# A two-layer AdaLN kernel: projection jobs of the attention stage behind its weightings, and token maxima spread by way of DRAM

## The chip, the cores and the metric

The kernel runs on one core of one Trainium2 chip. The metric is the device time of one execution in microseconds (us), a median over several runs. TensorE (PE) does the matrix products and the transposes, VectorE (DVE) and ScalarE (ACT) the elementwise work and the reductions, GpSimd (POOL) a few elementwise operations and the gathers. SyncE (SP) issues most of the transfers.

## The reference, cut to what matters

Two batches of 2048 tokens with 256 features go through two layers. The change lies in the two parts of the first layer.

```
# layer 0, attention: position i sees the positions j >= i - 16
h   = layernorm(x) * (1 + ca) + sa
q, k, v = h @ Wq.T + bq, h @ Wk.T + bk, h @ Wv.T + bv
att = softmax(where(j >= i - 16, q @ k.T / sqrt(256), -1e30))
x   = x + ga * ((att @ v) @ Wo.T + bo)

# layer 0, soft mixture: 8 experts of 128 slots
xn, se   = rms_norm(layernorm(x) * (1 + cb) + sb), rms_norm(slot_embeds)
logits   = xn @ se.T                       # per batch [2048 tokens, 1024 slots]
dispatch = softmax(logits, over the tokens)
combine  = softmax(logits, over the slots)
slots    = dispatch.T @ xn
y        = gelu(slots @ w1) @ w2
x        = x + gb * (combine @ y)
```

Behind it comes the second layer: a state-space block with a scan, then a mixture with a choice of tokens by each expert. The change leaves both alone.

## The kernel before, in words

The instructions of each engine are written out by hand, one program for each engine, and semaphores tie them together. An engine works through its own program in order. The program is cut into stages; the attention takes about the first 370 us of the span, the soft mixture the next 510 us.

**Attention (`attention`).** The rows of queries are cut into 32 tiles of 128, 16 for each batch, and taken from the last to the first, one in each step n from 0 to 31. Because a query sees all later keys, tile n of a batch sees 2 key tiles at first and 16 in the end. The kernel keeps scores in blocks of 512 keys, so a step has 1 to 4 blocks. In step n, PE does this, in order: the projection jobs of the step (`jobs_of(n)`), the transposes of the first three blocks of probabilities of row n (L469), the scores of row n + 1 (`scores`, into b_pS), and then the weightings of row n, one for each block (`weighted`, into b_pO), with the transpose of a fourth block behind the first of them. fp32 products are made of three products of high and low parts (`exact_matmul`, L61 to L63).

A job is something that PE puts into one of three slots of the PSUM tile b_pT and that is then taken out in two parts: ACT copies the high part (`high`), and DVE subtracts it from the same slot and keeps the low part (`low`). The kinds are "m" (modulation vectors, L369 and L371), "k" (a group of four tiles of h turned over, L408, low part on L661), "q" (low part on L663), "v" (low part on L668), "e" (slot embeddings turned over, L416, low part on L673) and "t" (a block of probabilities, high part on L544, low part on L676). Slots are used in turn: a job waits until the low part of the job three places earlier is out. A group's k jobs stand in step user - 3 and its q and v jobs in step user - 2, where user is the first step that reads the group. That gives these projection jobs: steps 0 to 3 have modulation jobs; steps 0, 4, 8, 13, 16, 20 and 24 have two k jobs; steps 1, 5, 9, 14, 17, 21 and 25 have two q and two v jobs; steps 27 to 30 have one e job each.

ACT does in step n: `high` of the projection jobs and of the first three blocks, the exponentials of row n + 1 (L553, which wait for DVE's maximum b_nmax), some squares, and `high` of a fourth block. DVE does in step n: `low` of the same jobs, the maxima of row n + 1 (`maxima`, L685 to L694), `low` of a fourth block, then side work that stands at fixed steps, and last `update` of row n (L700 to L707: reciprocal, row added to x, statistics), which waits for PE's last weighting. The side work is `group_scaled` (L622, steps 3, 7, 12, 15, 19, 23), `key_part` (L635 to L638, steps 2, 5, 9, 14, 17, 21, 25), `group_centred` (L614, steps 2, 6, 11, 14, 18, 22), `stats` (L715 to L725, steps 1, 4, 8, 10, 13, 16), and from step 24 `modulate` and `finish_row` of the rows of the next stage.

**Soft mixture (`soft_mixture`).** For each batch b the logits of all 8 experts are kept in SBUF (d_raw, 8 tiles of 128 slots by 2048 tokens). `tops` takes the maximum over the experts into d_top, so that what is left is a maximum over the 128 partitions for each token. For each half of 8 token tiles, PE transposes d_top into d_pT (`turn_tops`, L1811), DVE reduces it to one column for each tile (`row_tops`, L1231, into d_rmax), PE multiplies each column, spread over 128 columns, by the identity (`spread_tops`, L1818), and ACT copies the result back into d_top (L1582), where each partition now has the maxima of all tokens. DVE then subtracts d_top from the logits of each expert (`shift`, L1236), ACT takes the exponentials, and PE combines. Beside this chain PE works on the experts: `hidden` (8 tiles for experts 0 to 3, then 8 for 4 to 7) and `outputs` (one for each expert, into two halves of d_pO). `outputs` of expert et waits until DVE has taken expert et - 2 out (`processed`, L1240), and on DVE `processed(0)` stands behind `shift(0)`, `processed(1)` behind `shift(1)`, and so on. In batch 0 both `hidden` and `outputs` are products of high and low parts, in batch 1 plain fp32.

Of the kernel before, what the change touches and what calls it, by code (L numbers as in the profile page):

```python
# [4 lines left out]
F32 = mybir.dt.float32  # L5
# [7 lines left out]
P = 128  # L13
# [95 lines left out]
def attention(nc, m, w):  # L109
# [3 lines left out]
    with ExitStack() as ctx:  # L113
# [109 lines left out]

        jobs = [j for n in range(-1, NT) for j in jobs_of(n) + probs_of(n)]
        at = {j: i for i, j in enumerate(jobs)}
# [128 lines left out]
        def _(pe):  # L354
# [130 lines left out]
            for n in range(-1, NT):  # L485
                for job in jobs_of(n):
                    kinds[job[0]](job)
                    if job == ("m", 1, 0):
                        output_weights()
                probs = probs_of(n)  # L490
                for job in probs[:EARLY]:
                    transposes(job)
                if n + 1 < NT:
                    scores(n + 1)
                for i, job in enumerate(probs):
                    weighted(job)
                    if i + EARLY < len(probs):
                        transposes(probs[i + EARLY])

        @block.scalar  # L500
        def _(act):
# [70 lines left out]
            for n in range(-1, NT):  # L572
                probs = probs_of(n)
                for job in jobs_of(n) + probs[:EARLY]:
                    high(job)
                    if job == ("m", 1, 0):
                        act.wait_ge(s["fold_ps"], 1)
                        nc.scalar.copy(raw_wvo, by_two(pS[:, 0:GW])).then_inc(s["raw_done"], 1)
                        nc.scalar.copy(m.vrow[:], over(pS[:, GW:GW + C], B)).then_inc(s["raw_done"], 1)
                        nc.scalar.copy(wr[:], pS[:, GW + C:2 * GW]).then_inc(s["raw_done"], 1)  # L580
                    if job == ("k", 0, CH - 1):
                        weights_high(0)
# [4 lines left out]
                if SQUARES_AT <= n < SQUARES_AT + E:  # L587
# [4 lines left out]
                    nc.scalar.activation(junk[:], m.se[:, e], ACT.Square, accum_out=ss[:, e:e + 1]).then_inc(s["squared"], 1)  # L592
                for job in probs[EARLY:]:
                    high(job)
# [7 lines left out]
        def _(dve):  # L602
# [175 lines left out]
            for n in range(-1, NT):  # L778
                probs = probs_of(n)
                for job in jobs_of(n) + probs[:EARLY]:  # L780
                    low(job)
# [10 lines left out]
                if tiles_of_step(n - 2):  # L792
                    clamp(tiles_of_step(n - 2))
                for job in probs[EARLY:]:
                    low(job)
# [45 lines left out]
def soft_mixture(nc, m, w):  # L841

    with ExitStack() as ctx:
# [62 lines left out]
                                    for n, shape, o in (("uh", [P, 2, 2, C], 0), ("un", [P, 2, 2, C], 4 * 4 * C), ("ug", [P, 2, CH, 2 * P], 8 * 4 * C),  # L906
                                                        ("umod", [P, 3, C], 12 * 4 * C), ("ubout", [P, C], 15 * 4 * C))]
        third = placed("uh_third", [P, 2, C], area + 10 * KB)
        rows_of = lambda b, q: third[:] if b and q == PAIRS - 3 else uh_[b][:, q % 2]
# [10 lines left out]
                 "l_ready part_done max_done nmax_done exp_done raw_done top_done t_ready t_copied_a t_copied_d sl_ready rsum_done sl_scaled "  # L920
                 "h_ready h_done y_ready y_done ones_done mt_ready rmax_done mb_ready mb_done shifted p_done o_ready "
                 "crs_done x_done w_in x_out x_back st_done small_in mods_in u_bias u_chain u_pow "
# [69 lines left out]
        def _(sp):  # L992
# [11 lines left out]
            def turned_out(b, q):  # L1004
                await_copy(sp, at[b, "u", q, 0])
                cols = slice((b * NTB + 2 * q) * P, (b * NTB + 2 * q + 2) * P)
                sp.dma_start(m.uT_dram[:, :, cols], ug[b][:, q % 2]).then_inc(u_out[q % 2], 16)

            feed_forward(0)
            sp.wait_ge(s["x_out"], 16)  # L1010
            sp.wait_ge(s["y_ready"], E)
# [16 lines left out]
            for k in range(2):  # L1028
                sp.dma_start(wout[k][:], w["W_out"].rearrange("(k h p) n -> k p h n", p=P, h=2)[k]).then_inc(s["wout_in"], 16)
            for q in range(PAIRS - 3, PAIRS):  # L1030
                turned_out(0, q)
            for k in range(2):
                sp.wait_ge(u_out[k], 16 * PAIRS // 2)
# [98 lines left out]
        def _(dve):  # L1132
# [95 lines left out]
            def row_tops(b, h):  # L1228

                dve.wait_ge(s["mt_ready"], b * 2 + h + 1)  # L1230
# [175 lines left out]
            for b in range(B):  # L1406
# [45 lines left out]
                row_tops(b, 1)  # L1452
                for e in range(ES):
# [71 lines left out]
        def _(act):  # L1525
# [133 lines left out]
            for b in range(B):  # L1659
# [23 lines left out]
                for j in range(HT):  # L1683
                    gelu(b, 0, j)
                    if not b:
                        hidden_high(0, j)
                    if not b and j == 2:
                        slots_high_of(1)
                    if j == 4:
                        spread_tops(b, 0)  # L1690
                spread_tops(b, 1)
                if b:
# [35 lines left out]
        def _(pe):  # L1728
# [74 lines left out]
            def turn_tops(b, h):  # L1803
# [4 lines left out]
                else:  # L1808
                    pe.wait_ge(s["mb_done"], b * 2 + h)
                for t in range(NH):  # L1810
                    last = nc.tensor.transpose(pT[:, t // 4, t % 4 * P:(t % 4 + 1) * P], top[:, (h * NH + t) * P:(h * NH + t + 1) * P], m.ident[:])  # L1811
                last.then_inc(s["mt_ready"], 1)

            def spread_tops(b, h):
                pe.wait_ge(s["rmax_done"], b * 2 + h + 1)
                for t in range(NH):
                    col = h * NH + t
                    last = nc.tensor.matmul(pT[:, t // 4, t % 4 * P:(t % 4 + 1) * P], rmax[:, col:col + 1].to_broadcast([P, P]), m.ident[:],  # L1818
                                            start=True, stop=True)
                last.then_inc(s["mb_ready"], 1)  # L1820

# [47 lines left out]
            for b in range(B):  # L1869
# [34 lines left out]
                for j in range(HT):  # L1904
                    hidden(b, 0, j)
                    if j == 3:
                        spread_tops(b, 0)
# [4 lines left out]
                spread_tops(b, 1)  # L1912
# [1412 lines left out]
def program(nc, a, out):  # L3325
# [5 lines left out]
    m.y_dram = nc.dram_tensor("y_dram", [P, NT, C], F32).ap()  # L3331
    m.cum_dram = nc.dram_tensor("cum_dram", [NT * HEADS, P], F32).ap()
    m.bb_dram = nc.dram_tensor("bb_dram", [2, DT0], F32).ap()
    m.decayed = 2
# [114 lines left out]
```

## Time and profile before

| what | value |
|---|---|
| median of 3 runs | 1689.68 us (1688.67 to 1689.85) |
| profiled execution, its own time | 1690.98 us |
| span of the profiled execution | 1689.2 us |
| mean granted TensorE clock | 0.987 of full speed |
| PE busy | 1598.3 us, 95% |
| DVE busy | 1196.2 us, 71% |
| ACT busy | 779.8 us, 46% |

The profile is that of one execution. What it gives as busy is time in which an instruction of that engine ran; a PE instruction's end is modelled and overlaps the next one's start by up to 0.2 us, so the next start is the better mark. Times of instructions are microseconds from the start of the span, and 1.8 us of the execution's own time lie outside the span.

### The profile page before, as it was taken

What the parts mean: (1) busy time and instruction counts of PE and PEld (TensorE: products, weight loads), DVE (VectorE), ACT (ScalarE), POOL (GpSimd) and SP (SyncE); (2) the same over time, 40 slices, a digit from 0 to 9 for tenths busy, and PEclk for the clock granted to TensorE, in tenths of its full rate; (3) what the DMA queues carried; (4) which work ended last, traced back from release to release, by engine and by line L of the source; (5) the groups of instructions that cost most, each with busy time, mean ns of one, the idle gap of its engine ahead of it and who ended that gap; (6) DMA issues with size and microseconds to landing.
All of it is one profiled execution on the core that took longest, in us unless ns stands there. A gap on an engine that the chain in (4) does not pass through costs nothing. (4 is left out here: it accounts for less than half of the span.)

```text
span 1689.2 us, 25755 instructions
## 1 busy us (share of the span) xinstructions
PE 1598.3 (95%) x9282; PEld 1367.1 (81%) x9282; DVE 1196.2 (71%) x2655; ACT 779.8 (46%) x1529; POOL 582.0 (34%) x475
## 2 busy tenths in 40 slices
PE   6899989989999999999979999999889999999996
PEld 4689878888888888867867888888678778888896
DVE  6877688764567756646886898998877836666663
ACT  3333333344357134436237777778421314454542
POOL 2100020000000003322436777777400024777764
PEclk9999999999999999999988999999999999999999
DMA  7000000010010000111015222222241125565653
GB/s 230 5 1 1 1 1 1 1 51 1 1 50 4 23 13 20 66 57 69 28 59 207 73 91 78 78 79 82 69 149 51 50 65 172 136 168 144 147 119 38
DMA packets 80538, 113.14 MB, mean 67 GB/s; under 512 B 16014, under 2 KB 60186, under 8 KB 80028
## 3 DMA queue, kind: packets, MB, share of 16 engines
q1 hardware_dynamic: 66460, 93.00, 17.1%
q0 software_dynamic: 12288, 17.31, 5.7%
q8 instruction: 75, 1.23, 0.3%
q10 hardware_dynamic: 1664, 1.18, 0.2%
q14 instruction: 51, 0.42, 0.1%
HBM read 83.17 MB, written 27.68 MB: 66 GB/s over the span
## 5 line engine op out<-in xcount | busy, mean ns | idle before, releaser
L2001 POOL DMA_INDIRECT k_xe<-rows_dram,idx x64 | 82.3, 1286 | 179.0 <-DVE idx L3073 140.7
L3140 POOL DMA_INDIRECT out<-k_eo,idx x64 | 117.0, 1828 | 74.5 <-DVE k_eo L3236 57.3
L1830 PE MATMUL d_pO<-d_sp,d_raw 128*128 128x257 f32 x512 | 116.1, 384 | 1.9 <-DVE x L1248 1.7
L1830 PEld LDWEIGHTS d_pO<-d_sp,d_raw 128*128 128x128 f32 x512 | 96.8, 192 | 16.5 <-DVE x L1248 2.4
L553 ACT ACTIVATE b_p<-b_pS,b_nmax 128x384 f32<-128x384 f32 (+16 forms) x32 | 38.1, 1190 | 131.7 <-DVE b_nmax L694 131.7
L61 PE MATMUL b_pO<-b_vh,b_ph 128*128 128x256 f32 x302 | 87.8, 291 | 7.0 <-DVE b_pl L676 6.8
L62 PE MATMUL b_pO<-b_vh,b_pl 128*128 128x256 f32 x302 | 85.3, 282 | 0.0
L63 PE MATMUL b_pO<-b_vl,b_ph 128*128 128x256 f32 x302 | 85.3, 282 | 0.0
L347 POOL TENSOR_TENSOR x<-x,b_vrow 128x256 f32<-128x256 f32 x32 | 24.2, 786 | 168.8 <-DVE b_hs L622 168.7
L2217 ACT ACTIVATE g_dlm<-d_cumb,mod 128x128 f32<-128x128 f32 x256 | 78.5, 395 | 1.2 <-DMA d_cumb<-cum_dram 1.2
L3195 ACT ACTIVATE k_act_g<-k_pg 128x512 f32<-128x512 f32 x64 | 38.3, 599 | 87.3 <-PE k_pu L63 87.0
L3253 DVE TENSOR_TENSOR k_hid<-k_act_g,k_pu 128x512 f32<-128x512 f32 x64 | 44.0, 688 | 42.8 <-ACT k_act_g L3195 42.2
L1567 ACT COPY d_raw<-pL 128x512 f32<-128x512 f32 x64 | 37.3, 586 | 79.7 <-PE pL L63 79.7
L61 PE MATMUL k_po<-k_wh,k_hh 128*128 128x256 f32 x256 | 72.4, 283 | 0.6 <-issue 0.6
L63 PE MATMUL k_po<-k_wl,k_hh 128*128 128x256 f32 x256 | 72.5, 283 | 0.0
L62 PE MATMUL k_po<-k_wh,k_hl 128*128 128x256 f32 x256 | 72.4, 283 | 0.0
L2831 ACT ACTIVATE i_act_g<-i_pg 128x512 f32<-128x512 f32 x30 | 17.9, 598 | 114.2 <-PE i_pu L63 114.2
L676 DVE TENSOR_TENSOR b_pl<-b_pT,b_ph 128x512 fp32r<-128x512 f32 (+3 forms) x86 | 50.3, 618 | 24.0 <-ACT b_ph L544 24.0
L61 PE MATMUL b_pS<-b_kh,b_qh 128*128 128x512 f32 (+5 forms) x172 | 65.8, 383 | 1.4 <-DVE b_vl L668 1.4
L61 PEld LDWEIGHTS b_pO<-b_vh,b_ph 128*128 128x128 f32 x302 | 57.6, 191 | 10.5 <-DVE b_pl L676 10.2
L685 DVE TENSOR_REDUCE b_part<-b_pS 128x1 f32<-128x512 f32 (+4 forms) x86 | 49.8, 587 | 22.0 <-PE b_pS L63 21.8
L1118 POOL MEMSET d_sp<- 128x4 f32 x4 | 0.3, 105 | 181.8 <-PE pL L63 167.6
(583 smaller groups left out, 5495.5 us busy)
## 6 DMA issues: line engine op xcount, KB each, us to landing
d_cumb<-cum_dram SPq DMA_DIRECT2D x32, 512.0 KB, 4.2
k_wf<-in_WgT SPq DMA_DIRECT2D x16, 512.0 KB, 4.0
k_wf<-in_WuT SPq DMA_DIRECT2D x16, 512.0 KB, 4.9
k_wf<-in_WdT SPq DMA_DIRECT2D x16, 512.0 KB, 6.9
rows_dram<-h_hx SPq DMA_DIRECT2D x32, 136.0 KB, 3.9
x<-in_x SPq DMA_DIRECT2D x8, 512.0 KB, 10.4
d_w<-in_w SPq DMA_DIRECT2D x4, 1024.0 KB, 6.3
uT_dram<-d_ug SPq DMA_DIRECT2D x16, 256.0 KB, 2.4
```

What stands on the lines that cost most here:

```text
L61: nc.tensor.matmul(out, ah, bh, start=start, stop=False)
L62: nc.tensor.matmul(out, al, bh, start=False, stop=False)
L63: return nc.tensor.matmul(out, ah, bl, start=False, stop=stop)
L553: nc.scalar.activation(pr[:, n % 2, off:w], pS[:, bank[n] + off:bank[n] + w], ACT.Exp, bias=nmax[:, n % 2:n % 2 + 1], scale=scale, accum_o ...
L676: nc.vector.tensor_tensor(pl[:, r, 0:w], src[:, 0:w], ph[:, r, 0:w].bitcast(F32), ALU.subtract).then_inc(s["lo_done"], 1)
L685: nc.vector.reduce_max(part[:, n % 2, g:g + 1], pS[:, bank[n] + g * GW + skipped(n, g):bank[n] + g * GW + width(n, g)], axis=AX).then_inc( ...
L1830: last = nc.tensor.matmul(pO[:, t % 2, 0:PW], raw[e][:, t * P:(t + 1) * P], proc[e], start=e == 0, stop=e == E - 1)
L2001: nc.gpsimd.indirect_dma_start(out=m.xe[:, e % 2, t, :], out_offset=None, in_=m.rows, in_offset=bass.IndirectOffsetOnAxis(ap=column(m, e, ...
L2217: nc.scalar.activation(le[:, b, h, :], cumb[:, b, h, :], ACT.Relu, bias=cs[:, b, 3, h:h + 1], scale=-1.0).then_inc(s["dd_done"], 1)
L3140: nc.gpsimd.indirect_dma_start(out=out, out_offset=bass.IndirectOffsetOnAxis(ap=column(m, e, t), axis=0), in_=eo[:, e % 2, t, :], in_offse ...
L3195: nc.scalar.activation(act_g[:, f % 2], pg[:, f % 2], ACT.Gelu).then_inc(s["gelu_done"], 1)
L3253: nc.vector.tensor_tensor(hid[:, f % 2], act_g[:, f % 2], pu[:, f % 2], ALU.mult).then_inc(s["hid_done"], 1)
```

## The change

In the attention, the last projection jobs of a step move from the head of the step to behind its weightings, one behind each. The number of jobs that move is at most the number of blocks of the row. So in steps 3, 4, 8, 13, 14, 20, 24 and 27 to 30 all of them move, in steps 5 and 21 the two v jobs, in steps 9 and 25 all but the first q job, in steps 0, 1, 2, 16 and 17 only the last job. The three engines and the turn of the slots keep one common order. On ACT the moved jobs stand behind the exponentials of row n + 1, on DVE behind its maxima and ahead of the side work and the update.

In the mixture, PE's products with the identity and ACT's copies go (`spread_tops`). Both halves are now turned over and reduced early (the second behind the fourth `hidden` tile). PE turns d_rmax over with one transpose behind the seventh `hidden` tile, DVE keeps the 16 by 128 result in SBUF (`keep_tops`), and SP writes it to DRAM (8 KB) and, when that has landed, reads it back into all 128 partitions of d_top (1024 KB). `shift(0)` waits for that transfer. In batch 1 the two transfers stand on SP's queue ahead of the last turned pair (`turned_out(0, PAIRS - 1)`).

```diff
-        jobs = [j for n in range(-1, NT) for j in jobs_of(n) + probs_of(n)]
+        def ahead_of(n):
+            own, probs = jobs_of(n), probs_of(n)
+            return own[:max(len(own) - len(probs), 0)]
+
+        def between(n, i):
+            probs, later = probs_of(n), jobs_of(n)[len(ahead_of(n)):]
+            return probs[i + EARLY:i + EARLY + 1] + later[i:i + 1]
+
+        def behind(n):
+            return [j for i in range(len(probs_of(n))) for j in between(n, i)]
+
+        jobs = [j for n in range(-1, NT) for j in ahead_of(n) + probs_of(n)[:EARLY] + behind(n)]
...
@@ PE
-                for job in jobs_of(n):
+                for job in ahead_of(n):
                     kinds[job[0]](job)
...
                 for i, job in enumerate(probs):
                     weighted(job)
-                    if i + EARLY < len(probs):
-                        transposes(probs[i + EARLY])
+                    for later in between(n, i):
+                        if later[0] == "t":
+                            transposes(later)
+                        else:
+                            kinds[later[0]](later)
@@ ACT, and the same with low(job) on DVE
-                for job in jobs_of(n) + probs[:EARLY]:
+                for job in ahead_of(n) + probs[:EARLY]:
                     high(job)
...
-                for job in probs[EARLY:]:
+                for job in behind(n):
                     high(job)
@@ soft mixture, SP
+        token_tops = eT[0][0:NTB, 0:P]
+            def spread_tops(b):
+                sp.wait_ge(s["tops_kept"], b + 1)
+                sp.dma_start(m.tops_dram, token_tops).then_inc(s["tops_in"], 16)
+                sp.wait_ge(s["tops_in"], 32 * b + 16)
+                sp.dma_start(top[:], m.tops_dram.rearrange("t n -> (t n)").partition_broadcast(P)).then_inc(s["tops_in"], 16)
...
-            for q in range(PAIRS - 3, PAIRS):
+            for q in range(PAIRS - 3, PAIRS - 1):
                 turned_out(0, q)
+            spread_tops(1)
+            turned_out(0, PAIRS - 1)
@@ soft mixture, DVE
+            def keep_tops(b):
+                dve.wait_ge(s["mt_ready"], b * 3 + 3)
+                nc.vector.tensor_copy(token_tops, pT[0:NTB, 0, 0:P]).then_inc(s["tops_kept"], 1)
...
                 if e == 0:
-                    dve.wait_ge(s["mb_done"], (b + 1) * 2)
+                    dve.wait_ge(s["tops_in"], 32 * (b + 1))
@@ soft mixture, ACT
-            def spread_tops(b, h):
-                act.wait_ge(s["mb_ready"], b * 2 + h + 1)
-                nc.scalar.copy(top[:, h * HALF:(h + 1) * HALF], pT[:].rearrange("p s n -> p (s n)")).then_inc(s["mb_done"], 1)
@@ soft mixture, PE
-            def spread_tops(b, h):
-                pe.wait_ge(s["rmax_done"], b * 2 + h + 1)
-                for t in range(NH):
...
+            def turn_token_tops(b):
+                pe.wait_ge(s["rmax_done"], b * 2 + 2)
+                nc.tensor.transpose(pT[0:NTB, 0, 0:P], rmax[:], m.ident[:]).then_inc(s["mt_ready"], 1)
...
                     hidden(b, 0, j)
                     if j == 3:
-                        spread_tops(b, 0)
+                        turn_tops(b, 1)
+                    if j == 6:
+                        turn_token_tops(b)
                 if b:
                     pe.wait_ge(s["h_done"], b * SH * HT + HT)
-                turn_tops(b, 1)
-                outputs(b, 0)
-                spread_tops(b, 1)
-                for et in range(1, ES):
+                for et in range(ES):
                     outputs(b, et)
                 if b:
-                    pe.wait_ge(s["mb_done"], 2 * B)
+                    pe.wait_ge(s["tops_kept"], B)
```

## Rows read from the trace of the kernel before

**Rows 1.** The page, busy time, share of the span and instructions of each engine

```profile
PE 1598.3 (95%) x9282; PEld 1367.1 (81%) x9282; DVE 1196.2 (71%) x2655; ACT 779.8 (46%) x1529; POOL 582.0 (34%) x475
```

**Rows 2.** Busy time by stretches: start:end, length, then each engine's busy us

```profile
52.00:74.00 22.00, 18.16 (x104) 12.03 (x103) 19.63 (x63) 7.01 (x18) 4.97 (x6) 1.00 0.03 8
...
140.00:164.00 24.00, 24.00 (x173) 22.65 (x172) 15.13 (x42) 8.56 (x20) 0.00 (x0) 1.00 0.00 1
```

**Rows 3.** PE's waits from 0 to 390 us: in total, times, longest

```profile
PE b_pO L61 <- DVE b_pl L676: 6.8, 12, 1.4
PE b_pT L408 <- DVE b_hs L622: 4.8, 4, 1.4
PE b_pT L469 <- DVE o_sel L673: 4.6, 4, 1.8
PE b_pT L469 <- DVE b_kl L661: 3.8, 5, 1.3
...
PE b_pT L61 <- DVE b_kl L661: 1.7, 1, 1.7
```

**Rows 4.** Timeline of PE, steps 16 to 18: start, length, in brackets the idle before

```profile
221.22 0.39 PE L61 MATMUL b_pO<-b_vh,b_ph 128*128 128x256 f32 x1 [0.32 <-DVE b_pl L676]
...
223.21 0.63 PE L469 MATMUL b_pT<-ident,b_p 128*128 128x128 f32 x4 [0.66 <-ACT b_p L553]
...
226.15 0.39 PE L61 MATMUL b_pO<-b_vh,b_ph 128*128 128x256 f32 x1 [0.46 <-DVE b_pl L676]
```

**Rows 5.** Timeline of DVE in steps 16 and 17

```profile
213.21 0.21 DVE L694 TENSOR_SCALAR b_nmax<-b_lifted,b_along 128x1 f32<-128x1 f32 x1
213.34 1.40 DVE L715 BATCH_NORM_STATS2 st<-x 128x6 f32<-128x256 f32 x4
...
215.55 0.15 DVE L700 RECIPROCAL b_rden<-b_esum 128x1 f32<-128x1 f32 x1
...
216.87 1.40 DVE L663 SCALAR_TENSOR_TENSOR b_ql<-b_pT,qb,b_qh 128x512 fp32r<-128x512 f32 x2
```

**Rows 6.** Timeline of ACT in steps 16 and 17

```profile
210.02 1.07 ACT L523 CAST b_kh<-b_pT 128x512 fp32r<-128x512 f32 x2 [3.49 <-PE b_pT L408]
...
213.46 0.58 ACT L553 ACTIVATE b_p<-b_pS,b_nmax 128x384 f32<-128x384 f32 x1 [2.09 <-DVE b_nmax L694]
```

**Rows 7.** DVE by line, 0 to 370 us: busy us, mean ns, idle before

```profile
L704 DVE SCALAR_TENSOR_TENSOR x<-b_pO,b_rden,x 128x256 f32<-128x256 f32 x32 | 15.5, 484 | 11.4 <-PE b_pO L63 9.7 <-POOL x L347 0.8
...
L614 DVE SCALAR_TENSOR_TENSOR b_hs<-x,mean,mod 128x256 f32<-128x256 f32 x32 | 13.4, 481 | 0.2 <-DVE mod L647 0.2
...
L635 DVE SCALAR_TENSOR_TENSOR b_hw<-b_hs,wr 128x256 f32<-128x256 f32 x32 | 13.3, 471 | 0.0
```

**Rows 8.** Timeline of PE, the mixture in batch 1 and then in batch 0

```profile
741.77 1.95 PE L1818 MATMUL d_pT<-ident,d_rmax 128*128 128x128 f32 x16
...
751.27 1.09 PE L1811 MATMUL d_pT<-ident,d_top 128*128 128x128 f32 x8 [0.69 <-ACT d_work L1578]
...
761.37 7.17 PE L1795 MATMUL d_pO<-d_w,d_work 128*128 128x256 f32 x32 [0.31 <-DVE d_sp L1240]
...
515.31 0.39 PE L61 MATMUL d_pO<-d_w2h,d_hid_high 128*128 128x256 f32 x1 [0.94 <-DVE d_sp L1240]
```

**Rows 9.** Timeline of DVE, the first subtraction of each batch

```profile
512.63 2.29 DVE L1236 TENSOR_TENSOR d_raw<-d_raw,d_top 128x2048 f32<-128x2048 f32 x1 [3.19 <-ACT d_top L1582]
...
758.68 2.29 DVE L1236 TENSOR_TENSOR d_raw<-d_raw,d_top 128x2048 f32<-128x2048 f32 x1 [5.06 <-ACT d_top L1582]
```

**Rows 10.** Transfers: queue, count, KB each, median us from issue to landing

```profile
x<-x_dram SPq DMA_DIRECT2D x1, 1024.0 KB, 5.0
...
d_wide_bias<-in_b_in SPq DMA_DIRECT2D x1, 512.0 KB, 3.7
...
cum_dram<-d_cumT SPq DMA_DIRECT2D x1, 64.0 KB, 1.7
...
cum_dram<-d_cumT SPq DMA_DIRECT2D x1, 8.0 KB, 2.0
```

More of the change, by code:

```diff
@@ L779, in _ @@
                 probs = probs_of(n)
-                for job in jobs_of(n) + probs[:EARLY]:
+                for job in ahead_of(n) + probs[:EARLY]:
                     low(job)
@@ L793, in _ @@
                     clamp(tiles_of_step(n - 2))
-                for job in probs[EARLY:]:
+                for job in behind(n):
                     low(job)
@@ L920, in soft_mixture @@
                  "l_ready part_done max_done nmax_done exp_done raw_done top_done t_ready t_copied_a t_copied_d sl_ready rsum_done sl_scaled "
-                 "h_ready h_done y_ready y_done ones_done mt_ready rmax_done mb_ready mb_done shifted p_done o_ready "
+                 "h_ready h_done y_ready y_done ones_done mt_ready rmax_done tops_kept tops_in shifted p_done o_ready "
                  "crs_done x_done w_in x_out x_back st_done small_in mods_in u_bias u_chain u_pow "
@@ L1007, in turned_out @@
                 sp.dma_start(m.uT_dram[:, :, cols], ug[b][:, q % 2]).then_inc(u_out[q % 2], 16)
+            def spread_tops(b):
[3 more added lines that the diff above has]
+                sp.dma_start(top[:], m.tops_dram.rearrange("t n -> (t n)").partition_broadcast(P)).then_inc(s["tops_in"], 16)
             feed_forward(0)
+            spread_tops(0)
             sp.wait_ge(s["x_out"], 16)
@@ L1228, in row_tops @@
             def row_tops(b, h):
-                dve.wait_ge(s["mt_ready"], b * 2 + h + 1)
+                dve.wait_ge(s["mt_ready"], b * 3 + h + 1)
                 nc.vector.tensor_reduce(rmax[:, h * NH:(h + 1) * NH], pT[:].rearrange("p s (t n) -> p (s t) n", n=P), AX, ALU.max).then_inc(s["rmax_done"], 1)
+            def keep_tops(b):
+                dve.wait_ge(s["mt_ready"], b * 3 + 3)
+                nc.vector.tensor_copy(token_tops, pT[0:NTB, 0, 0:P]).then_inc(s["tops_kept"], 1)
             def shift(b, e):
                 if e == 0:
-                    dve.wait_ge(s["mb_done"], (b + 1) * 2)
+                    dve.wait_ge(s["tops_in"], 32 * (b + 1))
                 nc.vector.tensor_tensor(raw[e][:], raw[e][:], top[:], ALU.subtract).then_inc(s["shifted"], 1)
@@ L1451, in _ @@
                             slots_low(1)
-                row_tops(b, 1)
+                        if j == 3:
+                            row_tops(b, 1)
+                        if j == 5:
+                            keep_tops(b)
+                else:
+                    row_tops(b, 1)
+                    keep_tops(b)
                 for e in range(ES):
@@ L1688, in _ @@
                         slots_high_of(1)
-                    if j == 4:
-                        spread_tops(b, 0)
-                spread_tops(b, 1)
                 if b:
@@ L1808, in turn_tops @@
                 else:
-                    pe.wait_ge(s["mb_done"], b * 2 + h)
+                    pe.wait_ge(s["rmax_done"], b * 2 + h)
                 for t in range(NH):
@@ L1812, in turn_tops @@
                 last.then_inc(s["mt_ready"], 1)
-            def spread_tops(b, h):
-                pe.wait_ge(s["rmax_done"], b * 2 + h + 1)
-                for t in range(NH):
[L1817 to L1820, printed above, removed]
+            def turn_token_tops(b):
+                pe.wait_ge(s["rmax_done"], b * 2 + 2)
+                nc.tensor.transpose(pT[0:NTB, 0, 0:P], rmax[:], m.ident[:]).then_inc(s["mt_ready"], 1)
             def combine(b, t):
@@ L1906, in _ @@
                     if j == 3:
-                        spread_tops(b, 0)
+                        turn_tops(b, 1)
+                    if j == 6:
+                        turn_token_tops(b)
                 if b:
                     pe.wait_ge(s["h_done"], b * SH * HT + HT)
-                turn_tops(b, 1)
-                outputs(b, 0)
-                spread_tops(b, 1)
-                for et in range(1, ES):
+                for et in range(ES):
                     outputs(b, et)
                 if b:
-                    pe.wait_ge(s["mb_done"], 2 * B)
+                    pe.wait_ge(s["tops_kept"], B)
                     state_turn(0, PAIRS - 1)
@@ L3332, in program @@
     m.cum_dram = nc.dram_tensor("cum_dram", [NT * HEADS, P], F32).ap()
+    m.tops_dram = nc.dram_tensor("tops_dram", [NTB, P], F32).ap()
     m.bb_dram = nc.dram_tensor("bb_dram", [2, DT0], F32).ap()
```

## The prediction

> **What bounds the kernel now.** The page comes first: PE is busy for 95% of the span, DVE for 71% [rows 1], so an edit pays only where PE waits. The busy time by stretches shows two kinds of attention step: where a row has 13 or more key tiles, PE has no gap and DVE works 15.13 of 24 us; in the short rows of the start PE works 18.16 of 22 us and DVE 19.63 of 22 [rows 2]. There DVE is close to being the bound itself. The list of PE's waits names what the change aims at: 4.8 us for h scaled (L622), 4.6 for the e jobs' low parts, 3.8 for the k jobs' [rows 3], each because the transposes of a new row stand right behind projection jobs and need their slots. The biggest entry, 6.8 us for b_pl [rows 3], is PE ready to weight while DVE has not got to the low part of the probabilities. What keeps DVE from it is the DVE order: side work, update, then the low parts of the next row. For the mixture I read PE's timeline around L1818 and the first subtraction on DVE [rows 8, 9].
>
> **The attention: what is removed.** The moved work is the same work, no instruction more. What can go are the waits at projection jobs. Step 4's and 20's k jobs no longer stand ahead of DVE's scaled h, and in steps 27 to 30 the third transpose no longer waits for an e job: 4.6 us [rows 3], of which nearly all comes back, since there the e job is alone and has two or three weightings behind it.
>
> **The attention: what is added.** DVE now meets a moved job in the place of the fourth block, ahead of side work and update. In short rows that job's product runs on PE only behind the weighting, so DVE idles for it, and what stood in that gap before (side work) comes after. Who waits for it: the low parts of the next row behind the update, and behind them PE's next weighting. Three prices go into it. From the end of a job on PE to its low part out is 1.45 us: ACT 0.6 and DVE 0.7 with the handoffs (two ACT copies take 1.07 us [rows 6], two DVE low parts 1.40 [rows 5]; the one place in the trace where nothing hides it shows 1.65 [rows 3]). Side work: 2.2 for statistics (213.34 to 215.55 [rows 5]), four times 0.4 for centring, four times 0.43 for the key part (means of 481 and 471 ns that overlap the next [rows 7]). The update takes 1.05: 0.15 [rows 5], 0.48 [rows 7], and a statistics instruction, of which L715 has four in 1.40 [rows 5].
>
> Worked for steps 16 to 18. Before, DVE had b_nmax out at 213.42 and started the statistics at once [rows 5]. After, only one k job stands ahead, DVE is through with the maxima at 212.85, and PE weights from 211.75 (half a microsecond earlier) and turns the second k job over until 213.1. ACT takes the exponentials first (0.58 and 0.19 behind b_nmax [rows 6]) and a square of 0.6, so the copy runs until 214.65 and the low part is out at 215.35: DVE has stood idle for 1.85, and PE, which used to start the q jobs at 213.1, starts at 215.45. Behind it DVE needs 2.2 + 1.05 + 0.35 for statistics, update and slot scales (218.9), then four low parts of 2.55 in all: row 17's are out at 221.4, against 221.22 for the weighting before [rows 4]. The last v job now follows that weighting and ends at 224.05, and row 18 is turned over from there (223.21 before [rows 4]). In step 17 DVE idles again from 222.65 to 224.75, has v's low part at 225.4, and needs 1.75 + 1.05 + 0.4 + 0.6 for key part, update, embedding and low part: row 18 is weighted from 229.2 instead of 226.15 [rows 4]. Steps 16 to 18 lose 3.05 us.
>
> The same sum, step by step, gives for the other groups:
> - Steps 0 to 7: DVE idles 2.65, 2.1 and 1.7 us in steps 2, 3 and 4 behind m and k jobs and then has 3.35, 2.3 and 2.2 of side work; PE's q job of step 5 waits 1.9 for k's low part. Set against that are 1.05 us won by step 2 and the waits that go. Net 5.4 lost. These are the short rows where DVE had no room [rows 2].
> - Steps 8 to 10: q waits 0.7 for k, the third transpose of step 9 waits 1.6 for q's low part, which stands behind statistics and update; less 0.5 that goes. Net 1.9 lost.
> - Steps 13 to 15: four blocks a row. PE gains 3.1 us by step 15, but DVE has key part and centring (3.35) behind the last v job, so the first weighting of step 15 comes when it came before. Net 0.
> - Steps 20 to 23: the scaled-h wait goes (1.3), q waits 1.8 for k, key part and update come late, and with them maxima and exponentials of row 23. Net 2.25 lost.
> - Steps 24 to 30: 0.7 gained in step 24, used up by late DVE work in 26 (the exponentials of row 27 come 1.3 late), then 4.2 gained at the e jobs. Net 3.3 gained.
>
> Sum: 5.4 + 1.9 + 0 + 3.05 + 2.25 - 3.3 = 9.3 us slower. The bounds: if other gaps of DVE absorb half of each loss, 3; if every moved job costs PE the full 1.65 [rows 3], 13.
>
> **The mixture.** Each `spread_tops` is 16 PE instructions, 1.95 us [rows 8] with 1.8 to the next start; the ACT copy behind it, 1.0, is seen by PE only through `shift(0)`. Added are one transpose (0.15), a DVE copy of 16 by 128 (no row has it; between 0.15 for a column and 0.4 for 128x256, I take 0.25), and two transfers one behind the other. Writing 8 KB lands after 1.7 to 2.0 us, reading 1024 KB to the same layout after 5.0 [rows 10]. That the source is one row for all partitions shows no extra price: 512 KB of that kind took 3.7 [rows 10]. I take 1.8 + 5.2 with 0.2 for handoffs, 7.2; bounds 6.7 and 9. The Trainium skill (DMA: Bandwidth & Descriptors, section Anatomy of one DMA) gives an estimate of 2.0 us fixed plus bytes over 436 GB/s, 2.0 and 4.4 here; by it the sum would be 0.6 us better in each batch. Its fixed part agrees with the rows, its rate is better than the 5.0 us row.
>
> Batch 0: PE ends the fourth `hidden` tile at 498.7, turns the second half (0.95) and does three more tiles of 1.4, so it is through the seventh at 503.9. DVE keeps the maxima at 504.4, d_top is back at 511.6, against 512.63 [rows 9]. The third `outputs` product stands 2.68 behind that start (515.31 [rows 8]) and starts at 514.3. PE reached it 0.9 early before and now waits 2.7 there: the 3.5 us of products removed turn into waiting, 1.0 is gained. All that follows hangs on that product and shifts with it.
> Batch 1: the fourth tile ends at 741.77 [rows 8], the transposes take 0.95, three tiles 1.76 each; DVE has free hands, so the maxima are kept at 748.55 and d_top is back at 755.75 (758.68 [rows 9]). PE starts `outputs` without the transposes in front (751.27 [rows 8]) at 750.75, is through two at 3.45 each at 757.65, and goes on at 758.45 instead of 761.37 [rows 8]: 2.9 gained. SP is idle in both windows, and the transfer put behind waits for ACT until long after. Bounds: 0 and -1 with the slow transfers, 1.9 and 3.7 with the fast, so the mixture gives -1 to 5.6, taken as 4.0.
>
> **Sum.** 9.3 - 4.0 = 5.3 us slower than the profiled execution's 1690.98, which lies 1.3 above the median of the runs; against the median 1689.68, 1695.0.
>
> **The rivals.** A run of this kernel can tell about 0.2%, 3.4 us.
> - DVE's late side work is mostly absorbed: the losses of steps 0 to 23 halve to 6.3, less 3.3, and the mixture gives 4: 1 us faster, 1688.7. For it speaks that DVE idles 24 us in front of low parts over the stage; against it that the short rows have only 2.4 us of 22 free [rows 2]. Chance 0.22.
> - Faster: DVE finishes its side work before the low parts are needed. Then the waits for L622, L673 and L661 go (4.8 + 4.6 + 3.8 [rows 3]), k to q costs 1.5 in five steps, and the mixture gives 4: 1690 - 13.2 + 7.5 - 4 = about 1680. It decides from the point where side work, update and one low part (up to 5 us) fit into PE's transposes and scores; they take 2 to 3 us in the short rows and 6 to 7 in the long. Chance 0.15.
> - The transfers are slow, say 9 us in each batch (another read delayed on the same engines): PE waits at the third product, the mixture gives -1, the whole is 10 slower, 1700. The other transfers of this stage are over by then. Chance 0.08.
> - The forecast, 1691 to 1699: chance 0.55.
>
> **How the numbers follow.** The forecast's range comes from attention 5 to 12 and mixture 2.5 to 5. The first rival and the lower edge of the forecast lie within 0.2%: 0.22 and a seventh of 0.55, 0.30. Slower is 0.55, faster 0.15. From 1686 to 1700 leaves out the faster rival and the far end of the slow transfers.
>
> **What would show it.** In the trace after: DVE idles in front of L661, L668 and the modulation lines in steps 2 to 5, 8, 9, 16, 17, 20 and 21, and PE's waits for b_pl rise above 6.8 and those for b_kl at the first q product above 1.7, while those for b_hs and o_sel are gone. The attention ends some 9 us later, near 378. In the mixture, L1818 and L1582 are gone, PE waits about 2.7 us at the third product of batch 0 and 0.8 in batch 1, and the two transfers take about 7 us from `keep_tops`. The prediction is wrong if the stage ends no later than before, or if the read of 1024 KB takes far from 5 us.

## The result and the profile after

The changed kernel takes 1702.32 us (median of four runs, 1701.01 to 1705.55) against 1689.40 for the kernel before: ratio 1.0077, 95% interval [1.0065, 1.0089]. It is 12.9 us slower, where 5.3 were forecast, and the time lies above the forecast's 1691 to 1699. Timed once more on another chip, beside a kernel before of 1691.42, it took 1702.5 (1.0059 [1.0044, 1.0073]).

The profiled execution took 1701.01 us, its span is 1698.3, 9.1 longer than before. Read first: does the attention end later? The last update of a row on DVE (first line before, second after):

```profile
368.91 0.48 DVE L704 SCALAR_TENSOR_TENSOR x<-b_pO,b_rden,x 128x256 f32<-128x256 f32 x1 [1.44 <-PE b_pO L63]
```
```profile
381.88 0.48 DVE L720 SCALAR_TENSOR_TENSOR x<-b_pO,b_rden,x 128x256 f32<-128x256 f32 x1 [1.44 <-PE b_pO L63]
```

12.97 us later, against 9.3 forecast. So the stages behind gained 3.9, against 4.0. What PE waits for in the attention, to be held against [rows 3] (in total, times, longest):

```profile
PE b_pO L61 <- DVE b_pl L692: 14.3, 11, 3.9
PE b_pT L61 <- DVE b_kl L677: 8.6, 6, 2.1
PE b_pT L384 <- ACT b_cs L586: 7.3, 1, 7.3
PE b_pT L482 <- ACT b_p L569: 3.7, 5, 0.8
PE b_pS L61 <- DVE b_vl L684: 3.4, 4, 1.4
PE b_pT L482 <- DVE b_ql L679: 2.4, 3, 1.3
PE b_pT L482 <- DVE b_vl L684: 1.6, 3, 0.5
PE b_pT L421 <- DVE b_hs L638: 1.4, 1, 1.4
```

The waits that were to go went: b_hs from 4.8 to 1.4, o_sel from 4.6 to nothing. What came in their place is b_pl, 6.8 to 14.3, and b_kl in front of the first q product, 1.7 to 8.6. (L384 is the start of the kernel and is there before as well.) These are the waits that were forecast. But what came and what went do not add up to 13 us. The next view shows what is missing. PE's busy time in the whole stage, before and then after (start:end, length, the busy time of PE with its instructions and of the other engines, granted clock as a share of full, DMA share, GB/s):

```profile
0.00:370.10 370.10, 331.30 (x2196) 290.82 (x2196) 272.77 (x738) 133.51 (x272) 48.01 (x63) 1.00 0.09 28
```
```profile
0.00:383.10 383.10, 338.29 (x2196) 297.25 (x2196) 269.84 (x738) 131.97 (x272) 48.13 (x63) 0.97 0.08 27
```

The same 2196 instructions keep PE busy 7.0 us longer. Only 6.0 of the 13 us are idle time; the rest is slower work, and the third column from the end points to the reason: the granted clock is 0.97 instead of 1.00. Some of this lies ahead of the first moved jobs. In the first 45 us, before and after:

```profile
0.00:45.00 45.00, 29.52 (x132) 20.21 (x133) 28.05 (x81) 13.97 (x28) 12.31 (x22) 1.00 0.66 216
```
```profile
0.00:45.00 45.00, 32.57 (x133) 22.71 (x134) 27.94 (x81) 14.35 (x29) 12.29 (x22) 0.92 0.66 216
```

So 3.0 of the 7.0 us of slower work belong to the start and 3.9 to the rows behind it. Where the clock falls there is seen in PE's timeline at the two places that my sum for steps 16 to 18 was about:

```profile
211.84 0.58 PE L61 MATMUL b_pO<-b_vh,b_ph 128*128 128x256 f32 x1 [3.58 <-DVE b_pl L692]
212.22 0.42 PE L62 MATMUL b_pO<-b_vh,b_pl 128*128 128x256 f32 x1
212.44 0.42 PE L63 MATMUL b_pO<-b_vl,b_ph 128*128 128x256 f32 x1
...
214.14 0.41 PE L62 MATMUL b_pO<-b_vh,b_pl 128*128 128x256 f32 x1
214.36 0.41 PE L63 MATMUL b_pO<-b_vl,b_ph 128*128 128x256 f32 x1
...
226.05 0.47 PE L61 MATMUL b_pT<-b_kh,wqkh 128*128 128x512 f32 x1 [2.14 <-DVE b_kl L677]
```

PE stood 3.58 us for the low part of row 15, and then each product comes 0.21 us behind the one before. The twelve products of the block take 2.9 us. After the 2.14 us wait the products are slow too, from half a microsecond behind it, and the two q jobs and the v job of step 17 take 5.99 us (4.30 before). PE alone in slices of 2 us (busy time, granted clock, DMA share, GB/s):

```profile
212.00:214.00 2.00, 2.00 (x10) 0.50 0.00 0
214.00:216.00 2.00, 2.00 (x11) 0.50 0.00 0
216.00:218.00 2.00, 2.00 (x18) 0.91 0.00 0
226.00:228.00 2.00, 1.95 (x6) 0.65 0.00 0
228.00:230.00 2.00, 2.00 (x7) 0.50 0.00 0
230.00:232.00 2.00, 2.00 (x17) 0.99 0.00 0
```

0.50 is 1.2 instead of 2.4 GHz. The Trainium skill (TensorE: Matmul & The Clock Gate, Part 1) says that a gate sets PE's clock to half or full by how busy PE has been recently; these rows agree.

In the mixture, DVE's first subtraction of each batch answers to [rows 9], and the transfers to my term from [rows 10] (queue, size, us to landing; batch 0, then batch 1's read). The last two lines are PE's third product of batch 0 and of batch 1:

```profile
523.90 2.29 DVE L1266 TENSOR_TENSOR d_raw<-d_raw,d_top 128x2048 f32<-128x2048 f32 x1 [3.67 <-DMA d_top<-tops_dram]
...
767.30 3.16 DVE L1266 TENSOR_TENSOR d_raw<-d_raw,d_top 128x2048 f32<-128x2048 f32 x1 [6.04 <-DMA d_top<-tops_dram]
```
```profile
d_top<-tops_dram SPq DMA_DIRECT2D x1, 1024.0 KB, 4.9
tops_dram<-mod SPq DMA_DIRECT2D x1, 8.0 KB, 1.4
```
```profile
d_top<-tops_dram SPq DMA_DIRECT2D x1, 1024.0 KB, 4.6
```
```profile
526.58 0.39 PE L61 MATMUL d_pO<-d_w2h,d_hid_high 128*128 128x256 f32 x1 [2.71 <-DVE d_sp L1270]
...
770.85 7.17 PE L1824 MATMUL d_pO<-d_w,d_work 128*128 128x256 f32 x32 [0.32 <-DVE d_sp L1270]
```

1.4 and 4.9 us, in all 6.3 from the maxima kept (6.0 in batch 1), against 7.2 forecast. Counted from the end of the attention, the third product of batch 1 comes 3.5 us sooner (770.85 less 761.37 [rows 8], less 12.97).

### The profile page after: what moved, and what is told of

It reads as the page before. It is cut to its first block and busy times, and to the rows that moved or that the text cites. A ratio compares the mean times of both kernels' runs of the same rounds, so it can differ in the third digit from the quotient of the medians.

```text
span 1698.3 us, 25632 instructions
## 1 busy us (share of the span) xinstructions
PE 1598.1 (94%) x9220; PEld 1366.2 (80%) x9220; DVE 1192.5 (70%) x2657; ACT 775.0 (46%) x1525; POOL 577.6 (34%) x475
## 5 line engine op out<-in xcount | busy, mean ns | idle before, releaser
L61 PE MATMUL b_pO<-b_vh,b_ph 128*128 128x256 f32 x302 | 89.8, 297 | 14.4 <-DVE b_pl L692 14.3
L2632 PE MATMUL g_py<-g_wide,g_dlm 128*128 128x64 f32 x512 | 61.2, 273 | 0.8 <-POOL g_wide L2153 0.7
```

Of the source, the lines that this page charges most:

```text
L61: nc.tensor.matmul(out, ah, bh, start=start, stop=False)
L2632: last = nc.tensor.matmul(py[:, h * HD:(h + 1) * HD], mt[:, h, :], dtx[:, b, h * HD:(h + 1) * HD], start=True, stop=True)
```

## The experiments

Ratios are to the kernel before on the same chip. To compare stages I take one mark for each step, the start of the DVE instruction that adds a row to x (L704 before), and write down how much later than before it is in the profiled execution (us). The labels are those of the experiments below:

```
row updated   0     4     7    10    15    18    23    30    31   ends stage
changed     +1.2  +6.2  +7.7  +9.3 +10.8 +15.6 +17.6 +13.0 +13.0
e10 again   +3.2  +9.0 +10.5 +12.1 +13.5 +18.3 +20.4 +15.7 +15.7
e1 att.     +3.4 +11.5 +13.0 +14.6 +16.1 +20.9 +23.0 +18.3 +18.3
e8 filled   +0.3  +4.0  +5.5  +7.2  +6.6  +9.7 +11.8  +7.1  +7.1
e4 DVE      +0.1  -3.4  +0.3  +1.3  -1.6  +2.1  +2.8  -2.9  -2.9
e7 k ahead  +3.2  +5.3  +5.9  +6.8  +3.9  +3.3  +3.9  -1.1  -1.1
e5 chosen   +0.4  +1.6  +1.6  +1.6  -1.3  -1.3  -1.3  -7.2  -7.2
e3 e jobs   -0.3  -0.3  -0.3  -0.3  -0.3  -0.4  -0.4  -6.3  -6.3
e6 long     -0.3  -0.2  -0.3  -0.3  -3.1  -3.2  -3.2  -9.1  -9.1
e9 best     +0.7  -2.7  -2.7  -2.7  -5.6  -5.6  -5.6 -11.6 -11.6
```

**Each part alone** (e1, e2). The first seven hunks of the diff, and the others.

> The attention part alone, the mixture as before. The trace of the changed kernel has the attention ending 13.0 us later and the rest gaining about 4. If the two parts are independent, this kernel takes 1689.4 + 13 = 1702 to 1705 us, and with the mixture part alone the two differences add up to that of the whole change (12.9 us between the medians). Rival: the parts act on each other (a late attention changes when the mixture's loads land, or the granted clock of what follows); then this one would come out at the time of the whole change, 1702, or above 1707.

> The mixture part alone, the attention as before. By the prediction's term it gains 4.0 us: 1685.4. The traces so far show the first batch 1.7 us shorter up to the third output product, and a granted clock that falls after the wait in front of that product in the second batch. Rival: those clock losses eat the gain, and this kernel is within 1.5 us of 1689.4. A third product of batch 0 that waits 2.7 us and one of batch 1 that waits 0.3 to 0.8 would be the same in either case; what differs is the clock after them.

Measured: the attention part 1706.82 us (1.0093 [1.0078, 1.0108]), the mixture part 1687.31 (0.9983 [0.9971, 0.9995]), before 1690.39. +16.4 and -3.1 make +13.3, where the whole change gave +12.9: the parts are independent as far as these intervals can tell, which is some 3 us. The attention part lies above the 1702 to 1705 that I expected, the mixture part 1.9 us above its 1685.4. The mixture's gain is between 0.8 and 4.9 us by its interval, so its sign is confirmed, and 4.0 is not excluded. Its rival, that a lower clock eats the gain, falls: from 390 to 910 us the granted clock is 0.97 in the kernel before, in the changed kernel and in this one.

The attention part's runs spread over 6 us (1704.23 to 1710.43), and its profile, of the slowest of them, ends the stage 18.3 us late instead of 13.0. It shows one reason. Behind the same wait of 2.03 us in step 4, PE runs the same 26 instructions at full clock in the changed kernel (first line) and partly at half in this one (second):

```profile
80.00:85.00 5.00, 3.29 (x26) 1.00 0.10 28
```
```profile
84.00:89.00 5.00, 4.77 (x26) 0.66 0.11 28
```

So the same wait can cost the clock in one execution and not in another.

**Only the e jobs moved** (e3). In the changed kernel:

```
 own, probs = jobs_of(n), probs_of(n)
+if n < TURN_AT:     # 27
+    return own
 return own[:max(len(own) - len(probs), 0)]
```

> Only the e jobs of steps 27 to 30 are moved behind weightings, all other projection jobs stand ahead as before; the mixture part is in. The prediction had 4.2 us of gain at the e jobs and 4.0 in the mixture, and put all the loss into steps 0 to 26: 1681 to 1683. Rival 1: the e jobs' gain came only because rows 27 to 30 were late anyway; then 1685. Rival 2: moved jobs cost something at the e jobs as well: 1687 or more.

Measured 1681.19 (0.9945 [0.9932, 0.9957]), as expected. The stage ends 6.3 us sooner than before, 5.9 of it gained in steps 27 to 30. Where nothing late stands behind a moved job, the move pays more than the waits for o_sel had in the table (4.6).

**DVE's order** (e4). The one alteration to the changed kernel:

```
+side = True
 for job in behind(n):
+    if side and job[0] != "t":
+        side_work(n)      # group_scaled, key_part, group_centred, stats
+        side = False
     low(job)
...
-(the same four, behind the loop)
+if side:
+    side_work(n)
```

> The changed kernel with one order altered, on DVE alone: scaling, key part, centring and statistics of a step stand ahead of the low parts of its moved jobs instead of behind them. My theory: DVE idles in front of the moved jobs' low parts and does its side work afterwards, which makes the next row's low parts late. Then DVE's idle time is filled, the waits for b_pl fall from 14.3 to 6 us or less, the clock losses behind them go too, and the time is 1688 to 1693. Rival: what costs is that q waits for k's low part and a third transpose for q's, each right behind its product, so that PE stands still whatever DVE does beside it; side work in front makes these low parts later still, and the time stays at 1700 or rises to 1705.

Measured 1685.46 (0.9966 [0.9955, 0.9978]): some 17 us faster than the changed kernel by one order on an engine that is not the bound, and faster than before. PE's waits of the stage:

```profile
PE b_pT L61 <- DVE b_kl L677: 9.7, 6, 2.6
...
PE b_pO L61 <- DVE b_pl L692: 3.9, 8, 1.0
```

b_pl fell from 14.3 to 3.9. The waits for b_kl stayed, so the rival names a part of the loss, but the small one. The theory holds for the waits, and the time is below the 1688 to 1693 expected. The clock losses did not all go: behind two of the b_kl waits, of 2.19 and 2.65 us in steps 5 and 17, PE has a granted clock of 0.66 over the next 5 us.

**Waits filled** (e8). In the changed kernel PE multiplies something that nobody reads, ahead of four of its long waits; the result goes to a PSUM area that the row no longer needs.

```
+FILL = {3: 26, 4: 12, 15: 23}
+def fill(n, count):
+    start = bank[n] if short[n] else T // 2
+    for _ in range(count):
+        nc.tensor.matmul(pS[:, start:start + C], vh[:, key(n), 0:P], vh[:, key(n), :], start=True, stop=True)
...
 def weighted(job):
+    if g == 0 and n in FILL:
+        fill(n, FILL[n])
     pe.wait_ge(s["lo_done"], at[job] + 1)
...
 def query(job):
+    if (p, o) == (5, 0):
+        fill(16, 13)
```

> The changed kernel, its waits as they are, but PE runs products that nobody reads in four of them: 26 ahead of the weighting of step 3, 12 of step 4, 23 of step 15, and 13 ahead of the first q product of step 17 (waits of 3.93, 2.03, 3.58 and 2.14 us in the changed kernel's trace). Theory: of the 13 us that the attention lost, a part is no waiting but the granted clock, which falls to half behind these waits: busy time of PE up to the end of the stage is 338.3 us against 331.3 for the same instructions. With the waits filled the clock stays at full, the twelve products behind each wait take 1.6 us instead of 2.9 and the q and v jobs of step 17 4.6 instead of 6.0: 4 to 5 us faster than the changed kernel, 1697 to 1699. Rival: the slow products behind the waits have another cause (operands just written), and the extra work changes nothing or only delays: 1702 or more.

Measured 1695.38 (1.0026 [1.0016, 1.0036]), below the 1697 to 1699 expected. By the ratios that is 5.6 us less than the changed kernel's second timing (1.0059) and 8.6 less than its first (1.0077), for doing more work. In the profile the stage ends 5.9 us sooner than the changed kernel's; 0.9 of this is there when row 0 is updated, ahead of the first filled wait, so the filled waits are worth 5.0. The weighting of step 15, which had stood 3.58 us:

```profile
205.92 2.96 PE L492 MATMUL b_pS<-b_vh 128*128 128x256 f32 x23
209.66 0.39 PE L61 MATMUL b_pO<-b_vh,b_ph 128*128 128x256 f32 x1 [0.78 <-DVE b_pl L703]
209.88 0.28 PE L62 MATMUL b_pO<-b_vh,b_pl 128*128 128x256 f32 x1
...
210.12 0.28 PE L61 MATMUL b_pO<-b_vh,b_ph 128*128 128x256 f32 x1
```

0.12 us from product to product instead of 0.21. The operands were just as fresh, so the rival (a cost of fresh operands) falls. The twelve products are over 1.54 us behind their start (209.66 to 211.20, the next instruction's start) instead of 2.73 (211.84 to 214.57). The stretches around the filled waits, PE alone, first the changed kernel, then this one:

```profile
60.00:80.00 20.00, 14.35 (x72) 0.91 0.00 1
206.00:218.00 12.00, 7.90 (x50) 0.72 0.00 1
218.00:236.00 18.00, 15.20 (x94) 0.91 0.00 1
```
```profile
60.00:80.00 20.00, 18.57 (x120) 1.00 0.03 8
206.00:218.00 12.00, 11.15 (x89) 1.00 0.01 2
218.00:236.00 18.00, 14.37 (x96) 1.00 0.00 1
```

**The changed kernel again, unaltered** (e10).

> The changed kernel once more, unaltered, for more timed runs of it beside the kernel before, since its own runs reached from 1701 to 1705.6 us and the attention part alone went from 1704 to 1710. If the granted clock behind its long waits is chance from execution to execution, the profile shows other stretches at a lower clock than the first one, and the times spread over some us: a ratio of 1.007 to 1.010. If the clock falls at the same places each time, the attention ends 13 us late again within 1 us, and the spread has another source.

Measured 1702.5 (1699.2 to 1706.9). Both halves of the expectation came true in part. The clock falls at the same places as in the changed kernel's first profile:

```profile
60.00:80.00 20.00, 14.73 (x79) 0.91 0.00 1
206.00:218.00 12.00, 7.89 (x55) 0.76 0.00 1
218.00:236.00 18.00, 15.51 (x95) 0.87 0.00 1
```

But this execution, the slowest of its six, ends the stage 15.7 us late instead of 13.0. 2.0 of the 2.7 more are there when row 0 is updated, and the rest by row 1. The attention part alone and the kernel of the next experiment show the same late start in their profiled executions (+3.4, +3.2), the others do not. The clock goes with it: over the first 45 us it is 0.92 or 0.93 in these three and in the changed kernel's first profile (+1.2), and 0.96 to 1.00 in the eight others (-0.8 to +0.7). No experiment separates the two, so what makes the start late stays open. It is one source of the spread; the clock behind a wait of 2 us, above, is another.

**The k jobs ahead again** (e7). With DVE's new order, `if n in (4, 8, 16, 20, 24): return own` in `ahead_of`.

> Side work first on DVE, all jobs moved but the k jobs of steps 4, 8, 16, 20 and 24, which stand ahead of their step's scores as before. Theory: with side work first, what is left of the loss is that the first q product stands right behind the second k product, so that PE waits for the copy and k's low part (9.7 us in six places in the trace of side work first, against 1.7 before). Then most of the 12.7 us lost in steps 5, 9, 17, 21 and 25 comes back: 1675 to 1679 us, and the waits for b_kl at q fall to about 2. Rival: the loss in these steps comes from the moved q and v jobs (the third transpose behind q's low part, the scores behind v's): then 1683 to 1686.

Measured 1684.66 (0.9951 [0.9937, 0.9965]): my theory falls, except in one place. The waits for b_kl at q did fall, from 9.7 to 1.7 us. But by the marks of each row, side work first lost 1.9 us in step 9, 3.65 in step 17, 1.2 in step 21, 1.9 in step 25. With the k jobs ahead these are 1.5, -0.6, 1.0 and 2.3. So of these only step 17's loss came from the second k job; those of steps 9, 21 and 25 stay while the q and v jobs are moved. Step 5's loss fell from 4.05 to 0.9, but step 4, which had gained 0.9, lost 3.9 by something else, which the next kernel shows too. This profile is also one of those with a late start, so its time says less than its marks.

**Chosen steps** (e5, e6). DVE's new order, and jobs moved only in the steps of a list:

```
+MOVED = (0, 1, 2, 3, 13, 14, 27, 28, 29, 30)   # e5
+MOVED = (13, 14, 27, 28, 29, 30)               # e6
 own, probs = jobs_of(n), probs_of(n)
+if n not in MOVED:
+    return own
```

> Side work first on DVE, and jobs moved only in steps 0 to 3, 13, 14 and 27 to 30; the mixture part is in. In the trace of the kernel with side work first, the differences to the kernel before step by step are -3.4 us by step 4, then +4.05 in step 5, +1.9 in step 9, -2.9 in steps 13 and 14, +3.65 in step 17, +1.2 in step 21, +1.9 in step 25, and about -6 in steps 27 to 30. If the gains are where the moved jobs have nothing late behind them, and can be had without the losses, this kernel takes 1681.2 (e jobs alone) less 3.4 and 2.9: 1675 us. Rival: the early gains are no gains but are paid back at step 5, where the k jobs then stand in front of a row that came sooner; then 1678.

> As the one before, without the jobs of steps 0 to 3: moved only in steps 13, 14 and 27 to 30, where a row has four blocks. 1681.2 less 2.9: 1678.3. Rival: the gain of steps 13 and 14 is lost at the first short row behind them, as in the changed kernel (5.65 late at step 15's transposes, 8.7 at its weighting): 1681.

Measured: the first 1681.99 (0.9943 [0.9929, 0.9956]), later than both the 1675 expected and its rival's 1678; the second 1679.91 (0.9925 [0.9911, 0.9939]). The long rows give what was expected: 2.9 us in steps 13 and 14, kept through the short rows behind them. The early steps' 3.6 us by step 2 are lost in step 3 (1.4) and above all in step 4 (3.9), before the place that the rival named. ACT, PE and SP's queue in step 4 of the first kernel:

```profile
73.18 1.07 ACT L543 CAST b_kh<-b_pT 128x512 fp32r<-128x512 f32 x2 [4.54 <-DMA mod_dram<-o_vals]
```
```profile
74.54 0.69 PE L486 MATMUL b_pT<-ident,b_p 128*128 128x128 f32 x2 [3.42 <-DVE b_kl L681]
```
```profile
70.44 1.78 SPq L307 DMA_DIRECT2D mod_dram<-o_vals  x6
```

ACT may overwrite with k(2) only once the modulation vectors lie in DRAM, and SP stores them behind the last modulation job, m8 of step 3. With m8 behind a weighting the store is issued at 70.44, and ACT's copy of k(2), in order, waits for it; PE then stands for the low part. In the kernel before, the store was issued at 68.78 and the copy ran at 73.46 without waiting for it.

**m8 ahead again** (e9), all else as the first of the two (step 3 taken out of the list).

> Side work first, and jobs moved in steps 0 to 2, 13, 14 and 27 to 30; against the kernel with the chosen steps, the last modulation job (step 3) stands ahead of its scores again. In that kernel's trace ACT's copy of the first k job of step 4 waits 4.54 us for the stored modulation vectors, which are written out behind that modulation job; PE waits 3.42 us for k's low part, and the 3.6 us won by step 2 are lost in step 4. Theory: with the job ahead the store is early, that wait goes, and the gain of the first steps stays: attention 11 to 12 us shorter than before, 1675 to 1677 us on a chip whose before takes 1690. Rival: the first steps' gain is lost at the scaled h of the k jobs in any case, since DVE is the bound there: as without moved jobs in steps 0 to 3, ratio 0.9925, 1677 to 1679.

Measured 1675.52 (0.9907 [0.9891, 0.9922]), before 1691.42: the theory holds. It is 15.9 us faster than before and 27 faster than the changed kernel; the stage ends 11.6 us sooner than before. Of PE's waits only these are above 2 us, beside the start:

```profile
PE b_pT L425 <- DVE b_hs L642: 4.1, 3, 1.4
PE b_pT L486 <- DVE b_kl L681: 3.9, 5, 1.3
PE b_pO L61 <- DVE b_pl L696: 2.9, 8, 0.5
```

## Why the prediction was wrong

The direction was right, and so was the chain of waits; the size was not, because one cost was left out: 12.9 us lost, 5.3 forecast. By its own steps, with the marks above (changed kernel, then the one with filled waits, whose clock stays full in the attention from 27 us on):

- Steps 0 to 7, forecast 5.4 lost: 7.7 with the 1.2 of the start; with waits filled 5.2 from row 0 to row 7.
- Steps 8 to 10, forecast 1.9: 1.6 and 1.6.
- Steps 13 to 15, forecast 0: 1.4 lost; with waits filled 0.6 gained.
- Steps 16 to 18, forecast 3.05: 4.8; with waits filled 3.1.
- Steps 20 to 23, forecast 2.25: 2.1 and 2.1.
- Steps 24 to 30, forecast 3.3 gained: 4.7 gained in both. The e jobs give 5.9 where I put 4.2.

**The step that failed** is the one that prices what is added: "Three prices go into it". The price of a wait was its length. There was a fourth, the work behind the wait at half the clock, and the sum has no term for it. Filling four waits gave back 5.0 of 13.0 us; another 0.9 is the later start of the changed kernel's profile. What is left, 7.1, is less than the 9.3 that I had summed for waits, mainly for the e jobs. So the waiting was put 2.2 us too high, and the clock, 5.0, was left out. I had the clock column of before in hand, 1.00 in the stretches shown in [rows 2], and took it for a constant, though my own sum made PE stand for 2.35 us at the first q product of step 17 where no wait in [rows 3] is longer than 1.8.

That the stage ended 13.0 us late, just where the sum had its upper bound, is luck: the bound stood for waits of 1.65 us at every moved job and knows no clock, and with some thirty jobs moved in steps 0 to 26 that product is not 13 either. The text ahead of the sum also puts the 4.8 us of b_hs down to transposes of a new row; that entry is the k jobs themselves (L408) waiting for scaled h.

**The first rival** (side work absorbed) and the faster one fall for this order on DVE. The faster one named the right condition, side work done before the low parts are needed; with DVE's order altered its direction comes true (1685.46), its size, about 1680, not quite. The waits that it named went from 13.2 to 2.0 us, and k to q cost 8.0 where it put 7.5. **The rival of slow transfers** falls: they took 6.3 and 6.0 us, not 9.

**The mixture**: up to the third product of batch 0 I forecast 1.0 and it is 1.7 (526.58 less 515.31 [rows 8], less 12.97). Both batches together were put at 4.0: measured 3.5 up to the third product of batch 1, 3.9 over the rest of the profile, 3.1 alone. So batch 1 by itself gave 1.8 instead of 2.9. Two things in its rows took back more than the shorter transfers gave: ahead of the chain PE's granted clock is 0.79 from 743 to 751 us (1.00 before, from 735 to 751), and DVE's first subtraction takes 3.16 us instead of 2.29, with POOL at work beside it (in the kernel before, three later ones take 3.02 to 3.03 beside POOL's work, the others 2.3). The transfers were 0.9 and 1.2 shorter than my 7.2. Their estimate by the Trainium skill (DMA: Bandwidth & Descriptors, section Anatomy of one DMA), 2.0 and 4.4, has the sum about right (6.3 measured) and the parts not: 1.4 for 8 KB and 4.6 to 4.9 for 1024 KB. The section fits its rule to transfers issued by GpSimd, and these are SP's. DVE's subtraction waits 3.67 us for them in batch 0, and PE 2.7 in front of the third product, as forecast; in batch 1 PE waits 0.3 there instead of 0.8.

**The remaining difference.** The two profiled executions are 9.1 us apart in span and 10.0 in time, the medians 12.9. The rest is where each execution lies among its own: that of before is 1.6 us above its median, that of the changed kernel 1.3 below, and the second profile of the changed kernel is 6.6 us longer in span than the first. So of the 7.6 us by which the forecast was too small, 3.7 lie in the attention of this one profile (5.0 of clock and 0.9 of later start, less 2.2 of waits put too high), 0.1 in the mixture, 0.9 between span and time, and 2.9 in where the two executions lie.

## What to carry to other kernels

Where work is moved on the bound engine, look at the in-order queue of the engine that serves it: put what is ready beside it ahead of what must wait for the moved piece. Here that order alone was worth some 17 us. And move selectively: a job that something late hangs on (a store, the next job's operand, a short row's low parts) stays ahead, one that nothing hangs on goes behind. When a sum creates waits on PE that are longer than any in the trace of before, ask what the work behind them costs at half the clock, and read busy time of equal instructions in both traces to see it.

## What the runs showed of the hardware that was not expected

Behind PE waits of 3.93, 3.58 and 3.42 us in the attention, and from half a microsecond to 1.2 us behind waits of 2.14, 2.19 and 2.65, the granted clock was 0.50 for 3 to 4.5 us: 0.21 us from one 128x256 product to the next instead of 0.12. Twelve products then cost 1.2 us more, a third of the 3.58 us of the wait in front of them. A wait of 2.03 us in step 4 left it at 1.00 in two executions, and in a third (the attention part alone) the clock fell behind the same wait, so length alone does not decide. Products that nobody reads, run in the waits, kept the clock at 1.00 and made the kernel faster. In the kernel before, no wait of the attention but the first (7.6 us, at the start) is longer than 2.1 us, and its clock there is 1.00.
